# Third layer of a graph network: edge attributes of four groups in one load per stream, and row transposes right behind the second half step's first matmuls

## The reference

```python
def _L2_gnn_ref(x, edge_index, edge_attr, W1, b1, W2, b2):
    rol, col = (edge_index[0], edge_index[1])
    e_feat = jnp.concatenate([x[rol], x[col], edge_attr], axis=-1)
    h = jax.nn.relu(e_feat @ W1 + b1)
    v = h @ W2 + b2
    x_cand = jax.ops.segment_max(v, col, num_segments=num_nodes)
    return jnp.maximum(x_cand, x[:, -v.shape[-1]:])
...
x = _layernorm(x + _L2_gnn_ref(x, edge_index, edge_attr_32, ...), axis=-1)
```

## Time and profile before

| | |
|---|---|
| median of three runs | 20992.71 us (20983.97 to 21042.5) |
| profiled execution, its own time | 21020.92 us |
| its span | 21018.7 us |
| PE, DVE, ACT, POOL busy over the span | 62%, 53%, 15%, 56% |
| granted TensorE clock, mean over the span | 0.731 |

### The profile page before, as it was taken

One profiled execution on the slowest core, in us unless ns is written; L12 is line 12 of the kernel. 1 busy time (PEld: TensorE's weight loads), 2 busy tenths in 40 slices (PEclk: granted clock), 3 DMA queues, 4 the chain that ended last, 5 costly groups with the idle time before them and its releaser, 6 DMA issues. The chain is left out here.

```text
span 21018.7 us, 295438 instructions
## 1 busy us (share of the span) xinstructions
PE 13077.6 (62%) x92471; PEld 7366.7 (35%) x92471; DVE 11200.6 (53%) x19689; ACT 3071.4 (15%) x5120; POOL 11786.1 (56%) x10055
## 2 busy tenths in 40 slices
PE   0565555555554776676767652555555555699999
PEld 0344434333333444444444431212222112355554
DVE  2565544444444777777777773333322222567777
ACT  0222222222221111111111110111111111000000
POOL 4788888888885555555555554666666655100000
PEclk6565555555556888888888876666666666899999
DMA  7333333333333222222222213333333333489998
GB/s 276 47 40 37 37 38 39 38 37 37 38 38 46 48 48 46 47 48 46 47 45 48 46 40 34 71 72 70 73 71 71 70 71 69 128 258 291 290 292 266
DMA packets 3008049, 1817.19 MB, mean 86 GB/s; under 512 B 1739874, under 2 KB 2765227, under 8 KB 2988427
## 3 DMA queue, kind: packets, MB, share of 16 engines
q1 hardware_dynamic: 2211164, 1336.91, 24.3%
q0 software_dynamic: 669312, 166.80, 10.8%
q10 hardware_dynamic: 126512, 300.38, 4.1%
HBM read 1474.43 MB, written 392.90 MB: 89 GB/s over the span
## 5 line engine op out<-in xcount | busy, mean ns | idle before, releaser
L2005 POOL DMA_INDIRECT xg<-d_tab,s_i x3136 | 3256.6, 1038 | 2638.1 <-POOLq L1996 1646.2
L2545 POOL DMA_INDIRECT xg<-d_tab,s_i x3136 | 3001.6, 957 | 1901.5 <-POOLq L2541 951.9
L2265 PE MATMUL pR<-w,H 128*128 128x384 f32 x6272 | 2711.8, 562 | 1426.1 <-PEq L2259 799.8
L1403 POOL DMA_INDIRECT d_acc<-AG,ix x1568 | 2466.8, 1573 | 527.3 <-issue 458.7
L1403 POOL DMA_INDIRECT d_acc<-T,ix x1568 | 2467.2, 1573 | 478.1 <-issue 442.1
L2933 PE MATMUL pacc<-nodes,HB 128*32 128x512 fp8e4 x47040 | 2662.3, 380 | 48.9 <-PEq L2977 48.9
L2582 DVE TENSOR_TENSOR_SCAN U<-mU,U,up 128x512 f32<-128x512 f32 x392 | 501.6, 1279 | 3332.9 <-DVEq L2581 2748.1
L2265 PEld LDWEIGHTS pR<-w,H 128*128 128x128 f32 x6272 | 1231.3, 216 | 2554.7 <-issue 2204.3
L2705 PE MATMUL hb<-U,Wbc 128*128 128x512 f32 x784 | 645.5, 919 | 2217.8 <-PEq L2699 2047.3
L1756 PE MATMUL pm<-ms,eq 128*128 128x32 f32 x6272 | 1365.8, 399 | 888.4 <-PEq L1754 886.2
L2933 PEld LDWEIGHTS pacc<-nodes,HB 128*32 128x32 f16 x47040 | 1260.5, 97 | 1323.7 <-issue 62.9
(11 more groups left out here) (338 smaller groups left out, 17497.6 us busy)
## 6 DMA issues: line engine op xcount, KB each, us to landing
packed<-d_A SPq DMA_DIRECT2D x420, 1792.0 KB
row<-d_m SPq DMA_DIRECT2D x1568, 64.0 KB
xg<-d_tab,s_i POOLq DMA_INDIRECT x6272
wrow<-d_w SPq DMA_DIRECT2D x196, 512.0 KB
d_scan<-so ACTq DMA_DIRECT2D x392, 256.0 KB
d_A<-stage ACTq DMA_DIRECT2D x97, 784.0 KB, 3.3
d_ea<-in_ea_t ACTq DMA_DIRECT2D x1, 50176.0 KB
d_exp<-T ACTq DMA_DIRECT2D x1, 50176.0 KB, 250.8
```

Of the source, the lines that this page charges most:

```text
L1403: e.indirect_dma_start(out=d_acc[i], out_offset=bass.IndirectOffsetOnAxis(ap=ix[k][:, t:t + 1], axis=0), in_=mo[k][:, t * F:(t + 1) * F], ...
L2005: e.indirect_dma_start(out=xg[k][:, t, :], out_offset=None, in_=d_tab, in_offset=bass.IndirectOffsetOnAxis(ap=s_i[n][:, t:t + 1], axis=0)) ...
L2265: last = e.matmul(pR[u % 2][:, j, 0:384], H[k][:, (2 * u + j) * P:(2 * u + j + 1) * P], w2[:, :], start=True, stop=True)
L2545: e.indirect_dma_start(out=xg[n][:, j * ST + c, :], out_offset=None, in_=d_tab, in_offset=bass.IndirectOffsetOnAxis(ap=s_i[d][:, col:col + ...
```

## The change

Two things are changed, both in the third layer.

SP's loads into `ef`: instead of four buffers of one group there are two of a quad. The destination values of the four groups are still four DMAs; the attributes are one DMA for each stream over the whole quad, of the same 128-byte pieces. All are issued together, behind the quad's `fl`, which now frees this buffer too; `fw` is gone. Within a turn SP's order is sources, `ef`, `mU`, `row`, `kt`, where it was `kt`, sources, `mU`, `row`, `ef`. PE waits for `ef` once a quad.

PE's order: `features` of the next group is called inside the second half step, behind its two `hb` matmuls and ahead of `turn`, where it stood at the half step's end, behind the counting matmuls.

```diff
-            ef = [sb(edges, f"ef{n}", [P, CH, 2, P]) for n in range(DEEP)]
+            ef = [sb(edges, f"ef{d}", [P, 4 * CH, 2, P]) for d in range(2)]
...
-                    def load_edges(a_, w):
-                        e.wait_ge(S(f"fw{w}"), 1)
-                        e.sem_inc(S(f"fw{w}"), -1)
-                        e.dma_start(ef[w][:, :, :, 0:64].rearrange("p j q x -> p (j q) x"),
-                                    exp_v[bass.ds(a_ * 4 + w, 1), :, :, :].rearrange("a p (n c) f -> (a p) n (c f)", c=2)
-                                    ).then_inc(S(f"le{w}"), 16)
+                    def load_edges(a_, d):
+                        for w in range(4):
+                            e.dma_start(ef[d][:, w * CH:(w + 1) * CH, :, 0:64].rearrange("p j q x -> p (j q) x"),
+                                        exp_v[bass.ds(a_ * 4 + w, 1), :, :, :].rearrange("a p (n c) f -> (a p) n (c f)", c=2)
+                                        ).then_inc(S(f"le{d}"), 16)
                         for c in range(ST):
-                            e.dma_start(ef[w][:, :, c // 2, 64 + F * (c % 2):64 + F * (c % 2 + 1)],
-                                        ea32_v[c, bass.ds(a_, 1), :, w * CH * F:(w + 1) * CH * F]
-                                        .rearrange("a p (j f) -> (a p) j f", f=F)).then_inc(S(f"le{w}"), 16)
+                            e.dma_start(ef[d][:, :, c // 2, 64 + F * (c % 2):64 + F * (c % 2 + 1)],
+                                        ea32_v[c, bass.ds(a_, 1), :, :].rearrange("a p (j f) -> (a p) j f", f=F)
+                                        ).then_inc(S(f"le{d}"), 16)
...
                     def chunk(c, n, at):
                         for d in range(2):
+                            load_sources((c - MID) * 2 + 1 + d, 1 - d)
+                            load_edges((c - MID) * 2 + 1 + d, 1 - d)
+                            load_rows((c - MID) * 2 + 1 + d, 1 - d)
                             count_load(e, A, at, n, d)
-                            load_sources((c - MID) * 2 + 1 + d, 1 - d)
-                            load_rows((c - MID) * 2 + 1 + d, 1 - d)
-                            for w in range(4):
-                                load_edges((c - MID) * 2 + 1 + d, w)
...
                     def turn(r, q):
-                        n = r % 4
-                        if q == 0:
-                            e.wait_ge(S(f"le{n}"), 80)
-                            e.sem_inc(S(f"le{n}"), -80)
+                        n, d = r % 4, r // 4
+                        if q == 0 and n == 0:
+                            e.wait_ge(S(f"le{d}"), 128)
+                            e.sem_inc(S(f"le{d}"), -128)
...
-                        else:
-                            e.sem_inc(S(f"fw{r % 4}"), 1)
-                            if r % 4 == 3:
-                                e.sem_inc(S(f"fl{r // 4}"), 1)
+                        elif r % 4 == 3:
+                            e.sem_inc(S(f"fl{r // 4}"), 1)
                         e.matmul(hb[q][:, :], Wbc[:, :], U[k][q][:, :], start=True, stop=False)
                         e.matmul(hb[q][:, :], Wa[64 * q:64 * (q + 1), :], XT[64 * q:64 * (q + 1), :], start=False, stop=True
                                  ).then_inc(S("hz"), 1)
+                        if count is not None:
+                            features((r + 1) % 8, count)
                         if not last:
                             turn(r if q == 0 else (r + 1) % 8, 1 - q)
```

More of the change, by code:

```diff
@@ L2455, in _ @@
                         e.sem_inc(S(f"fl{d}"), 1)
-                    for n in range(DEEP):
-                        e.sem_inc(S(f"fw{n}"), 1)
                     def load_sources(a_, d):
@@ L2504, in _ @@
                     e.sem_inc(S("past_" + e.engine.name), 1)
+                    load_edges(0, 0)
                     load_rows(0, 0)
-                    for w in range(4):
-                        load_edges(0, w)
                     def chunk(c, n, at):
                         for d in range(2):
+                            load_sources((c - MID) * 2 + 1 + d, 1 - d)
+                            load_edges((c - MID) * 2 + 1 + d, 1 - d)
+                            load_rows((c - MID) * 2 + 1 + d, 1 - d)
                             count_load(e, A, at, n, d)
-                            load_sources((c - MID) * 2 + 1 + d, 1 - d)
-                            load_rows((c - MID) * 2 + 1 + d, 1 - d)
-                            for w in range(4):
-                                load_edges((c - MID) * 2 + 1 + d, w)
                     over_chunks(e, LATE, chunk)
@@ L2521, in _ @@
                         e.sem_inc(S(f"fl{d}"), -1)
-                    for n in range(DEEP):
-                        e.wait_ge(S(f"fw{n}"), 1)
-                        e.sem_inc(S(f"fw{n}"), -1)
                     finish["sp"](e)
@@ L2668, in turn @@
                     def turn(r, q):
-                        n = r % 4
-                        if q == 0:
-                            e.wait_ge(S(f"le{n}"), 80)
-                            e.sem_inc(S(f"le{n}"), -80)
+                        n, d = r % 4, r // 4
+                        if q == 0 and n == 0:
+                            e.wait_ge(S(f"le{d}"), 128)
+                            e.sem_inc(S(f"le{d}"), -128)
                         for j in range(CH):
-                            last = e.transpose(up[:, j * P:(j + 1) * P], ef[n][:, j, q, :], ident[:, :])
+                            last = e.transpose(up[:, j * P:(j + 1) * P], ef[d][:, n * CH + j, q, :], ident[:, :])
                         last.then_inc(S("up"), 1)
@@ L2691, in second, with step @@
                             last.then_inc(S("tp"), 1)
-                    def step(r, q, first=False, last=False):
+                    def step(r, q, first=False, last=False, count=None):
                         k = r % 2
@@ L2716, in chunk @@
                         for i in range(16):
-                            step((i // 2 + 2) % 8, i % 2)
+                            step((i // 2 + 2) % 8, i % 2,
+                                 count=(c - MID) * 512 + ((i // 2 + 3) // 4 + 1) * 256 if i % 2 else None)
                             for w in range(2 * i - 2, 2 * i + 2 if i == 15 else 2 * i):
@@ L2720, in chunk @@
                                     count_sums(e, A, n, w)
-                            if i % 2:
-                                features((i // 2 + 3) % 8, (c - MID) * 512 + ((i // 2 + 3) // 4 + 1) * 256)
                     turn(0, 0)
@@ L2726, in _ @@
                     step(0, 0, first=True)
-                    step(0, 1, first=True)
-                    features(1, 256)
+                    step(0, 1, first=True, count=256)
                     step(1, 0)
-                    step(1, 1)
-                    features(2, 256)
+                    step(1, 1, count=256)
                     over_chunks(e, LATE, chunk)
                     step(2, 0)
-                    step(2, 1)
-                    features(3, G // 4 * 256)
+                    step(2, 1, count=G // 4 * 256)
                     step(3, 0)
```

## The result

The changed kernel is slower: 21,429.6 us (21,420.6 to 21,462.0), the kernel before on the same chip 20,999.7 (20,984.0 to 21,042.5), ratio 1.020, interval 1.018 to 1.022. That is 430 us more, where 290 less was forecast and 20,150 to 21,030 us was the range.

A forecast was written before the change was run, and what follows sets the result against it. The third layer's loop was taken as bound by POOL's gathers plus pauses for late PE signals. Saving 5.7 us on each of 49 quads, 279 us, gave 20,742 us profiled, 20,710 us median; range 20,150 to 21,030.

The forecast's parts named there:

- The bound: Third layer's edge loop: a group is 20.16 us of gathers plus a 4.86 us pause, POOL awaiting PE.
- The XT copies: Third layer's loop: expected to start in the middle of gathers in three groups of four.
- the pair in the earlier trace: Two third-layer groups before the change, 48.54 us; less 2.0 for indices, 46.54, or 23.27 for each group without loads.
- the sum: Third layer's quad: 3 x 23.27 + 24.5 = 94.3 us, now 100.0; over 49 quads 279 us saved.
- the moved transposes, put at zero beyond what the pair contains: PE's earlier row transposes: 0.60 us before up, at most 118 us over 196 groups; no net effect taken.
- a state that a load or store during a run of gathers brings on: Claimed cause of late PE signals in the third layer, lasting until about 3 us after the gathers pause.
- the half of the gain that rested on fewer loads: SP's 30 DMAs a quad become 18, leaving three groups of four nearly free of loads, at 23.27 us each.
- Rival B: Third layer: gathers or ACT's store keep signals late, a group stays 25.0 us, nothing moves: 20,990 us; chance 0.16.
- Rival C: Third layer: early XT starts a second group's gathers with PE work left; pauses 12.3 us, 21,180 us; chance 0.16.
- 0.69 to faster: Whole kernel: combined chance of a faster result, against same 0.16 and slower 0.15.
- The two small costs that were put at zero: Third layer: transposes' 0.60 us before up, at most 118 us; key loads behind the block, possibly 48 us.
- Rival A: Third layer: POOL becomes the bound, gathers run without pause at 20.16 us a group: 20,070 us; chance 0.18.

The follow-up runs named there:

- the table: Changed kernel with a small POOL instruction and wait behind every 8th, 4th, 2nd or each gather: 21,140.2, 20,779.3, 21,154.7, 22,182.0 us; paces 1.33, 1.41, 1.57, 1.90 us.

## Why the prediction was wrong

*The bound was read rightly.* POOL waits for PE, PE for signals; signals come after the gathers pause. The XT copies did move into the gathers, as foretold.

*The step that failed: "If the three groups behave as the pair in the earlier trace rows ... a group [takes] 23.27".* In that pair XT happened to come among the gathers, and one pause of 7.30 us followed. I took its 46.54 us for what every pair with an early XT takes. It measured about 55. In the terms of the sum: the moved transposes, put at zero beyond what the pair contains, cost 2.2% by themselves, and the loads, which were to bring such pairs about, gave 0.3%. Making XT early for sure changes which signal is late, not that one is: U's comes from the up transposes, and a group has two of them. The pause behind the 74 pairs has a median of 15.5 us, against 9.7 for two pauses of before: 74 times 5.8 us is 429 of the 440 us by which the loop grew.

*The cause was read wrongly: "a state that a load or store during a run of gathers brings on".* Without the scan's stores, in a run of gathers with no transfer from SP or ACT, signals were as late. So the half of the gain that rested on fewer loads wasn't there. The loads alone gained 52 us by the medians (ratio 0.997), and a quad's four groups took 24.4 to 25.7 us on average, none of them 23.27. Rival B, nothing moves, comes nearest to what that half of the change did.

*Rival C had the mechanism and the side, with too small a price.* Its pause was 2.9 us and 1.5 half steps at PE's usual speed, 12.3. Measured in the pair above are one half step, but of 8.55 us with the clock at its lower level instead of 6.3, and the signal 5.4 us behind the last gather, of a run twice as long, instead of 2.9. It was also applied to three groups of four; pairs went on across quads. Its sign, pauses above 10 us, is what the profile shows (82 of 195). I gave it 0.16, and 0.69 to faster: too much weight on one pair that fitted.

*The two small costs that were put at zero* can't have decided: the moved transposes' 0.60 us ahead of up (at most 118 us of the 430) and the keys behind the block (48 us kept). These runs don't separate them, but the loads alone, with the keys last, were no slower.

*Rival A's end (POOL without pauses at 20.16 us a group)* wasn't reached: at a pace of 1.25 us the signals were late in every kernel here, and the best is 23.5 to 23.8 us a group, with the break.

## What to carry to other kernels

When an engine waits for signals that all come after another engine pauses, making one of them early moves the wait to the next; ask what is second in line, and how much work is left when the pause comes. A run of two groups that fits a forecast is an outcome, not a price: look for what the runs that don't fit have in common. And try slowing the engine that crowds the others: a break of 0.65 us behind every fourth gather gained more than either edit.

## What the runs showed of the hardware

While POOL issues these gathers 1.25 us apart, PE's completion signals are late. In the kernel before, of the waits for PE whose work ended in the first 7 us of a run, at most 3% in any microsecond were over 0.5 us late; at 10 us it was 71%, from 11 us on over 90%. In the changed kernel it was 74% at 7 us already.

After runs of 16 gathers (146 of them, kernel before) the first late wait ends 3.1 us behind the last gather, after runs of 32 (49, changed kernel) 5.4 us; the changed kernel's own runs of 16 (38) have 3.4. That is 0.13 to 0.19 us for each gather. An estimate from it is that something works off a gather in 1.38 to 1.44 us and that PE's signals wait for it; the table's turn between 1.33 and 1.57 us agrees. The estimate has limits that these runs don't explain. Runs of 64 to 96 gathers at the loop's start had the first late wait end 0.3 to 7.5 us after them, which isn't in proportion. And the up of 15564.44 was heard while the gathers ran on, so waiting until all of them are worked off isn't the whole of it.

The DMA engines were not full: from 14372 to 14385, with hardly anything but gathers running, their mean share was 9 to 11%. The Trainium skill, Perfetto Trace Analysis, section "DMA Instruction — SWDGE (GPSIMD)", says that such an instruction's record ends when the last of POOL's cores has generated its descriptors, not when the data has moved. That leaves room for work behind the 0.95 us rows; no run here shows which part of it holds PE's signals up, and that stays open.

The Trainium skill, TensorE: Matmul & The Clock Gate, section "The cost: per-tile semaphore tail", gives some 26 ns for an increment. The trace leaves room for that where gathers start 1.57 us apart and more (no U or XT is over 0.2 us late), and not where they are 1.25 us apart (XT 10.6 us late in the median, kernel before).
